# FP4 rounding from exponent bits, and one pass of each feed-forward pair on GpSimd

## The chip, the core and the metric

The kernel runs on one core of a Trainium2 chip. The metric is the device time of the whole kernel in microseconds. Before the change it took 3304.03 us (median of 3 runs, 3299.87 to 3309.81).

## What is computed

The kernel computes two layers of a small network on 4 x 1024 tokens of width 128. The change concerns the feed-forward part of layer 0, which works on FP4 values:

```python
_GRID = [0.0, 0.5, 1.0, 1.5, 2.0, 3.0, 4.0, 6.0]
_MID = [0.25, 0.75, 1.25, 1.75, 2.5, 3.5, 5.0]
def fp4_quant_dequant(x):                  # blocks of 16 along the last dimension
    xb = x.reshape(shape[:-1] + (shape[-1] // BLOCK, BLOCK))
    scale = jnp.max(jnp.abs(xb), axis=-1, keepdims=True) / 6.0
    scale = jnp.maximum(scale, 1e-12)
    xn = xb / scale
    idx = jnp.searchsorted(_MID, jnp.abs(xn))
    q = _GRID[idx] * jnp.sign(xn) * scale
...
gate = fp4_linear(x, w_gate)               # both operands are quantized
y = fp4_linear(x, w_up)
h = jax.nn.silu(gate) * y                  # 352 hidden values a token
return fp4_linear(h, w_down)
```

The input x is the layer-normed hidden state. Around this stand a gated delta-rule attention (layer 0), a causal attention and a mixture of eight experts (layer 1).

## The kernel before

The program is written out engine by engine, with semaphores between the engines; each engine works through its instructions in the written order, and nothing is planned at run time. Stages end in `end_phase`, where every engine drains and waits for all others. Everything that changes lies in the first stage.

The 4096 tokens lie as 32 tiles of 128 (tokens on the partitions), so `xn` and `xq` are 128 x 4096. VectorE normalizes x (`layernorm`), then quantizes all of x in one call of `quantize` (L562) into `xq`, raises `xq_done`, and quantizes the weights (`wraw`, 128 x 1120) into `wqt` in a second call. For x, ScalarE has written the sizes and signs into `fa` and `fsg`; for the weights VectorE makes them itself (L2174 to L2177). Once `xq_done` is up, GpSimd clears `bias3` with a memset (L1599) and splits the bias (L1602 to L1606); it has no other work until the next stage.

TensorE turns the weights (L1698, L1701) and then works through 16 pairs of tiles. For pair p: transposes of `xn` and `xq` (L1711, L1713), ScalarE's copies of them (L1982, L1983), the matmuls of gate and up (L1720, the gate half first), ScalarE's silu of the gate (L1986), VectorE's product with up (`hid`, L2187), the quantization of `hid` on VectorE into `hq` (128 x 704), with sizes and signs from ScalarE (L1991, L1994), the transposes of `hq` (L1747), ScalarE's copies (L2011, L2012), the down matmuls (L1753), and the addition into the residual `res` (L2191, `add_down`). The gate logits of the next stage ride along (L1729, L1732, copied at L1998, L1999).

The order is staggered by one pair: TensorE does gate and up of pair p+1 ahead of turning `hq` of pair p, and VectorE adds pair p-1's result into `res` inside the quantization of pair p, ahead of the sign product. After the second to last pair, VectorE adds the biases for the gates (L2212, L2214) and ScalarE computes a sigmoid over all gate logits and a root (L2019 to L2023), with two loads of function tables; it does so after its copies of that pair's turned hidden values.

`quantize` takes 13 passes: maximum of each block, scale, reciprocal, product with the reciprocal (L571), comparison with 5.0 (L573), two fused comparisons and additions (L575), doubling (L576), four more comparisons (L578), product with half the sign (L580), product with the scale (L581). Each pass waits for the one before by a semaphore (`link`).

Of the kernel before, what the change touches and what calls it, by code (L numbers as in the profile page):

```python
# [10 lines left out]
ALU = mybir.AluOpType  # L11
# [23 lines left out]
LEVELS = 3  # L35

# [25 lines left out]
def layer_kernel(nc, a, out):  # L62

    ctx = ExitStack()
    with ctx:
# [56 lines left out]
        fsg = sb("fsg", [P, T * D], scope=s1)  # L122
# [1467 lines left out]
        def _(pool):  # L1590
# [15 lines left out]
            split.done(pool.tensor_copy(bias_h[:, 2, :], bias_r[:, 1, :]))  # L1606
            end_phase(pool)
# [85 lines left out]
        def _(pe):  # L1693
# [11 lines left out]
            def gate_up(p):  # L1705
# [8 lines left out]
                last.then_inc(x_turned, 1)  # L1714
                pe.wait_ge(xT_done, 2 * p + 2)
# [19 lines left out]
            gate_up(0)  # L1735
            gate_logits(0)
            for p in range(FP):
                if p + 1 < FP:
                    gate_up(p + 1)
                    gate_logits(p + 1)  # L1740
                pe.wait_ge(hq_done, p + 1)
                pe.wait_ge(hT_done, 2 * p)
                pe.wait_ge(ffn_added, p)
                for y in range(2):
                    for c in range(3):
                        w = min(P, INNER - P * c)
# [219 lines left out]
        def _(act):  # L1966
            act.wait_ge(var_done, 1)
            act.activation(stats[:, 0, :], stats[:, 1, :], ACT.Sqrt).then_inc(std_done, 1)
            act.wait_ge(norm_done, 1)
            act.activation(fa[:, :], xn[:, :, :].rearrange("p t d -> p (t d)"), ACT.Abs).then_inc(sign_done, 1)  # L1970
            act.activation(fsg[:, :], xn[:, :, :].rearrange("p t d -> p (t d)"), ACT.Sign).then_inc(sign_done, 1)
# [7 lines left out]
            def begin_pair(p):  # L1979
# [3 lines left out]
                act.copy(xnT[:, 2 * P * p:2 * P * p + 2 * P], bank[0][:, 0:2 * P]).then_inc(xT_done, 1)  # L1983
                act.wait_ge(gu_done, 2 * p + 1)
# [3 lines left out]
            def sizes(p):  # L1988
                act.wait_ge(hid_done, p + 1)
                act.wait_ge(hq_done, p)  # L1990
                act.activation(fa[:, 0:2 * INNER], hid[:, :, :].rearrange("p y w -> p (y w)"), ACT.Abs).then_inc(hsign_done, 1)  # L1991

            def signs(p):
                act.activation(fsg[:, 0:2 * INNER], hid[:, :, :].rearrange("p y w -> p (y w)"), ACT.Sign).then_inc(hsign_done, 1)  # L1994
# [6 lines left out]
            begin_pair(0)  # L2001
            sizes(0)
            signs(0)
            keep_logits(0)
            for p in range(FP):
                if p + 1 < FP:
                    begin_pair(p + 1)
                    sizes(p + 1)
                act.wait_ge(h_turned, p + 1)
                act.wait_ge(down_done, p)  # L2010
                act.copy(hqT[:, :, 0:2, :], turn2[:, :, 0:2 * P].rearrange("p y (c w) -> p y c w", c=2)).then_inc(hT_done, 1)  # L2011
                act.copy(hqT[0:INNER - 2 * P, :, 2, :], turn2[0:INNER - 2 * P, :, 2 * P:3 * P]).then_inc(hT_done, 1)  # L2012
                if p + 1 < FP:
                    signs(p + 1)
# [146 lines left out]
        def _(dve):  # L2161
# [5 lines left out]
            quantize(dve, seq, xf, T * D // BLOCK, fa[:, :], fc[:, :], fsg[:, :], fsc,  # L2167
                     xq[:, :, :].rearrange("p t d -> p (t d)"),
                     lambda: dve.wait_ge(sign_done, 1), lambda: dve.wait_ge(sign_done, 2)).then_inc(xq_done, 1)
# [3 lines left out]
            wneg = fa[:, NW:2 * NW]  # L2173
            seq.link(dve.tensor_scalar(wneg, wraw[:, :], 0.0, None, ALU.is_lt))  # L2174
            seq.link(dve.scalar_tensor_tensor(out=fsg[:, 0:NW], in0=wraw[:, :], scalar=0.0, in1=wneg,
                                              op0=ALU.is_gt, op1=ALU.subtract))
            seq.link(dve.tensor_tensor(fa[:, 0:NW], wraw[:, :], fsg[:, 0:NW], ALU.mult))  # L2177
            quantize(dve, seq, wraw[:, :], NW // BLOCK, fa[:, 0:NW], fc_top, fsg[:, 0:NW], fsc,
                     wqt[:, :], lambda: None, lambda: None).then_inc(wq_done, 1)
# [3 lines left out]
            def hidden(p):  # L2183
                dve.wait_ge(silu_done, p + 1)
                dve.wait_ge(gu_done, 2 * p + 2)
                dve.wait_ge(hsign_done, 2 * p)
# [7 lines left out]
            for p in range(FP):  # L2194
                dve.wait_ge(hid_done, p + 1)
                dve.wait_ge(hq_done, p)

                def sign_ready():
                    if p:
                        add_down(p - 1)  # L2200
                    dve.wait_ge(hsign_done, 2 * p + 2)

                def abs_ready():
                    dve.wait_ge(hsign_done, 2 * p + 1)
                    dve.wait_ge(h_turned, p)
                quantize(dve, ffn, hid[:, :, :].rearrange("p y w -> p (y w)"), 2 * INNER // BLOCK, fa[:, 0:2 * INNER], fc_top[:, 0:2 * INNER],
                         fsg[:, 0:2 * INNER], fsc, hq[:, :, :].rearrange("p y w -> p (y w)"), abs_ready, sign_ready).then_inc(hq_done, 1)
# [330 lines left out]
```

## Time and profile before

| | |
|---|---|
| median of the timed runs | 3304.03 us |
| span of the profiled execution | 3302.8 us |
| VectorE busy | 2513.2 us (76%) |
| TensorE busy | 2799.4 us (85%) |
| ScalarE busy | 1627.2 us (49%) |
| GpSimd busy | 1339.6 us (41%) |

The page's busy times are averages over all stages. The stage of the change is the first one and ends near 323 us. The page states one time for the profiled execution, its span; the three timed runs are other executions. A busy time adds up the durations of instructions; consecutive linked instructions start 0.03 us after the one before has ended, and an instruction that does not wait for the one before it can start before that one's end.

### The profile page before, as it was taken

How to read it: one execution, taken by the hardware profiler on the slowest of the kernel's cores; microseconds unless marked ns; L12 is line 12 of the kernel's file. 1: busy time of each engine (PE TensorE's matmuls, PEld its weight loads, DVE VectorE, ACT ScalarE, POOL GpSimd, SP SyncE). 2: the span in 40 equal slices, each digit the busy share in tenths (PEclk: the TensorE clock that was granted, in tenths of full speed). 3: DMA queues.
4: the chain of work that ended last, by engine and by line, in shares of the span. 5: the costliest groups of instructions: out<-in, count | busy, mean ns of one | idle time of the engine just before them, and what ended most of it. 6: DMA issues, size and time to landing. Idle time of an engine off the chain costs nothing. (4 is left out here: it accounts for less than half of the span.)

```text
span 3302.8 us, 74706 instructions
## 1 busy us (share of the span) xinstructions
PE 2799.4 (85%) x27685; PEld 1932.7 (59%) x27685; DVE 2513.2 (76%) x4548; ACT 1627.2 (49%) x3792; POOL 1339.6 (41%) x2151
## 2 busy tenths in 40 slices
PE   0466999675999999999999999999867488888888
PEld 0354444464777777777777777777656372222223
DVE  8898788794787868788687877876577467877775
ACT  1233999684434334443434334344366355555555
POOL 0000223312565655656566565655564504311111
PEclk9887999897999999999999999999889689999999
DMA  1000665686123242232323233133187321111111
GB/s 58 1 0 24 227 237 239 250 267 158 34 75 67 44 86 62 57 68 69 52 67 81 43 77 70 43 73 70 44 279 226 126 55 36 35 24 21 20 28 28
DMA packets 487649, 290.82 MB, mean 88 GB/s; under 512 B 402899, under 2 KB 447507, under 8 KB 478483
## 3 DMA queue, kind: packets, MB, share of 16 engines
q1 hardware_dynamic: 478070, 256.64, 28.8%
q10 hardware_dynamic: 4608, 16.78, 1.6%
q0 software_dynamic: 4608, 12.59, 1.1%
q8 instruction: 225, 3.69, 0.5%
q14 instruction: 138, 1.13, 0.1%
HBM read 155.92 MB, written 129.99 MB: 87 GB/s over the span
## 5 line engine op out<-in xcount | busy, mean ns | idle before, releaser
L2457 DVE TENSOR_REDUCE mx<-banks 128x2 f32<-128x1024 f32 (+3 forms) x384 | 358.2, 956 | 106.5 <-PE banks L1882 84.9
L2148 ACT ACTIVATE probs<-banks 128x1024 f32<-128x1024 f32 (+3 forms) x384 | 306.9, 810 | 246.1 <-PE banks L1904 239.1
L1131 ACT COPY xs<-banks 64x64 f32<-64x64 f32 (+2 forms) x640 | 166.1, 260 | 397.3 <-PE banks L963 394.2
L832 POOL TENSOR_SCALAR xc<-xc,halves 128x64 f32<-128x64 f32 (+1 forms) x256 | 192.3, 751 | 360.9 <-DVE xc L1311 348.3
L1686 POOL TENSOR_SCALAR_AFFINE_SELECT probs<-probs 128x256 f32<-128x256 f32 x256 | 103.7, 407 | 523.9 <-ACT probs L2148 523.7
L963 PE MATMUL banks<-xc,ssm 64*64 64x16 f32 (+2 forms) x5120 | 250.3, 217 | 36.5 <-issue 34.6
L963 PEld LDWEIGHTS banks<-xc,ssm 64*64 64x64 f32 x5120 | 209.8, 135 | 115.8 <-issue 57.0
L1761 PE MATMUL banks<-wproj,xnT 128*128 128x512 f32 x512 | 265.3, 600 | 0.6 <-DVEq L484 0.6
L1311 DVE SCALAR_TENSOR_TENSOR xc<-xc,halves,banks 64x64 f32<-64x64 f32 (+1 forms) x512 | 159.9, 312 | 111.5 <-PE banks L974 105.4
L1121 ACT COPY ssm<-banks 16x64 f32<-16x64 f32 (+2 forms) x896 | 215.9, 241 | 50.8 <-PE banks L935 38.6
L1156 ACT COPY ah<-banks 128x768 f32<-128x768 f32 x128 | 102.2, 798 | 254.8 <-PE banks L995 254.8
L1620 POOL TENSOR_TENSOR prj_sq<-prj 128x1024 f32<-128x1024 f32 x32 | 77.5, 2423 | 368.6 <-ACT prj L2032 368.6
L995 PE MATMUL banks<-stk,tw 128*128 128x192 f32 x1024 | 204.8, 344 | 0.5 <-DVE tw L1309 0.5
L1904 PE MATMUL banks<-q_less,k_parts 64*128 64x512 bf16 (+3 forms) x768 | 134.0, 346 | 80.8 <-DVE mx L2457 61.2
L1921 PE MATMUL banks<-probs,vaug 128*9 128x256 f32 (+3 forms) x1920 | 195.7, 449 | 0.0
L985 PE MATMUL banks<-S_t,kqt 64*128 64x128 f32 x2048 | 184.6, 299 | 0.3 <-issue 0.3
L839 POOL TENSOR_TENSOR ag<-ah,gt_sb 128x512 f32<-128x512 f32 x128 | 162.9, 1273 | 49.7 <-ACT ah L1156 49.5
L995 PEld LDWEIGHTS banks<-stk,tw 128*128 128x128 f32 x1024 | 166.2, 193 | 16.0 <-DVE tw L1309 0.7
L974 PE MATMUL banks<-xs,ttw 64*64 64x32 f32 (+1 forms) x3072 | 171.2, 224 | 0.5 <-ACT xs L1131 0.5
L1147 ACT ACTIVATE nycv<-banks 128x512 f32<-128x512 f32 x128 | 76.4, 597 | 181.3 <-PE banks L985 181.3
L974 PEld LDWEIGHTS banks<-xs,ttw 64*64 64x64 f32 x3072 | 139.3, 135 | 44.3 <-ACT xs L1131 43.8
L1761 PEld LDWEIGHTS banks<-wproj,xnT 128*128 128x128 f32 x512 | 96.6, 192 | 98.5 <-issue 48.1
(361 smaller groups left out, 6768.5 us busy)
## 6 DMA issues: line engine op xcount, KB each, us to landing
proj_s<-prj SPq DMA_DIRECT2D x32, 2048.0 KB, 6.8
qkv_t<-proj_s SPq DMA_DIRECT2D x32, 1536.0 KB
ka<-proj_s ACTq DMA_DIRECT2D x32, 512.0 KB, 4.8
mem_s<-o_sb SPq DMA_DIRECT2D x32, 512.0 KB, 2.6
om<-mem_s SPq DMA_DIRECT2D x32, 512.0 KB, 3.9
om<-proj_s SPq DMA_DIRECT2D x32, 512.0 KB, 4.8
nblk_s<-ssa POOLq DMA_DIRECT2D x32, 256.0 KB, 4.6
blk_s<-res SPq DMA_DIRECT2D x16, 512.0 KB, 4.0
```

Source lines behind the costliest of these rows:

```text
L832: pool.tensor_scalar(inverse_of(k, lv + 1)[:, :, w:2 * w], inverse_of(k, lv), halves[:, lv, 1:2], None, ALU.mult).then_inc(half_set, 1)
L839: pool.tensor_tensor(ag[:, :, :], ah[:, k % 2, :, 0:P], gt_sb[:, k % 2, :, :], ALU.mult).then_inc(ag_set, 1)
L963: last = pe.matmul(products(k, lv, out_)[right, w * m:w * m + w], ssm[rows, lv, m, right], inverse_of(k, lv)[rows, m, :], start=True, stop ...
L974: last = pe.matmul(updates(k, lv, out_)[right, w * m:w * m + w], turned[right, right], xs[right, k % 2, w * m:w * m + w], start=True, stop ...
L985: last = pe.matmul(cols(bk[2 + m % 2], 2 * w + p), kqt[r, k % 2, p, w, :], S_t[r, 2 * g + p, :], start=(w == 0 and p == 0), stop=(w == 0), ...
L995: last = pe.matmul(cols(bk[p], m % 2, P + DK), tw[:, k % 2, m, :], stk[:, k % 2, m, :], start=True, stop=True)
L1121: last = act.copy(ssm[rows, lv, :, right].rearrange("p (k e) t -> p e k t", e=2), both[rows, :, :, right])
L1131: last = act.copy(xs[right, k % 2, 0:4 * (SUB << lv)], products(k, lv, out_)[right, :])
L1761: pe.matmul(bank[n], xnT[:, P * i:P * i + P], wproj[:, 512 * n:512 * n + 512], start=True, stop=False)
L1921: last = pe.matmul(bank[6][row:row + SLOT, n0 * P:512], vaug[:, b * TB + j, 2 * (s % 8) + e, :], p_, start=(j == 0), stop=(j == 6 + odd))
L2148: act.activation(probs[:, s % 2, :, at:at + w], slot_of((kind, s, k))[:, :, 0:w], ACT.Exp, scale=D1 ** -0.5).then_inc(b_read, 1)
L2457: dve.tensor_reduce(mx[:, s % 2, c, :, t:t + 1].rearrange("p e a -> p (e a)"), slot_of((kind, s, k))[:, :, 0:w], AX, ALU.max).then_inc(a_r ...
```

## The change

A new function `round_blocks` takes the place of `quantize`. It multiplies the signed value by 1/scale and by a constant just under 1 (so that ties go down), takes the exponent bits of the result with a bitwise AND, which gives a power of two, takes the larger of that and 1.0 times 1.5 * 2^22, adds this number and subtracts it again. The addition rounds to the grid of the number's binade. No size and no sign is needed, so ScalarE's Abs and Sign go, and VectorE's three passes for the weights' signs. The product with the scale is a function of its own, `scaled`. For x and the weights it stays on VectorE; for the pairs GpSimd does it. `fa` and the scales get two halves for this, used in turn. The semaphore `hsign_done` now says that a pair's rounding is done.

The order in the loop changes too. TensorE goes: turn `hq` of pair p-1, gate and up of p+1, down of p-1, turn x of p+2, gate logits of p+1. VectorE adds the residual of pair p-1 after the rounding of p. ScalarE's block of sigmoid and root keeps its place at the end of turn p = FP-2, but the copies of that pair's turned hidden values are now in the turn after it.

```diff
+I32 = mybir.dt.int32
+EXPONENT = 0x7F800000
+ROUNDER = 1.5 * 2 ** 22
+TIES_DOWN = 1.0 - 2.0 ** -22
...
-        def quantize(dve, c, src, n, a_, acc, sgn, sc, dst, abs_ready, sign_ready):
+        def round_blocks(dve, c, src, n, y, step, sc):
...
             c.link(dve.reciprocal(inv, scale))
-            abs_ready()
-            c.link(dve.tensor_tensor(blocks(a_), blocks(a_), inv.unsqueeze(2).to_broadcast([P, n, BLOCK]), ALU.mult))
-
-            c.link(dve.tensor_scalar(acc, a_, 5.0, 2.0, ALU.is_gt, ALU.mult))
-            for mid in (3.5, 2.5):
-                c.link(dve.scalar_tensor_tensor(out=acc, in0=a_, scalar=mid, in1=acc, op0=ALU.is_gt, op1=ALU.add))
-            c.link(dve.tensor_scalar(acc, acc, 2.0, None, ALU.mult))
-            for mid in (1.75, 1.25, 0.75, 0.25):
-                c.link(dve.scalar_tensor_tensor(out=acc, in0=a_, scalar=mid, in1=acc, op0=ALU.is_gt, op1=ALU.add))
-            sign_ready()
-            c.link(dve.scalar_tensor_tensor(out=acc, in0=acc, scalar=0.5, in1=sgn, op0=ALU.mult, op1=ALU.mult))
-            return dve.tensor_tensor(blocks(dst), blocks(acc), scale.unsqueeze(2).to_broadcast([P, n, BLOCK]), ALU.mult)
+            c.link(dve.scalar_tensor_tensor(out=blocks(y), in0=blocks(src), scalar=TIES_DOWN, in1=inv.unsqueeze(2).to_broadcast([P, n, BLOCK]), op0=ALU.mult, op1=ALU.mult))
+            c.link(dve.tensor_scalar(step.bitcast(I32), y.bitcast(I32), EXPONENT, None, ALU.bitwise_and))
+            c.link(dve.tensor_scalar(step, step, 1.0, ROUNDER, ALU.max, ALU.mult))
+            c.link(dve.tensor_tensor(y, y, step, ALU.add))
+            return dve.tensor_tensor(y, y, step, ALU.subtract)
+
+        def scaled(eng, y, n, sc, dst):
...
+            return eng.tensor_tensor(blocks(dst), blocks(y), sc[:, 0, 0:n].unsqueeze(2).to_broadcast([P, n, BLOCK]), ALU.mult)
...
 # GpSimd, behind the splitting of the bias
+            for p in range(FP):
+                pool.wait_ge(hsign_done, p + 1)
+                pool.wait_ge(h_turned, p)
+                scaled(pool, pair_of(fa, p), NPB, scales_of(p), hq[:, :, :].rearrange("p y w -> p (y w)")).then_inc(hq_done, 1)
...
 # TensorE
-            gate_up(0)
-            gate_logits(0)
-            for p in range(FP):
-                if p + 1 < FP:
-                    gate_up(p + 1)
-                    gate_logits(p + 1)
...
+            turn_x(0)
+            gate_up(0)
+            turn_x(1)
+            gate_logits(0)
+            for p in range(FP + 1):
+                if p >= 1:
+                    turn_hidden(p - 1)
+                if p + 1 < FP:
+                    gate_up(p + 1)
+                if p >= 1:
+                    down(p - 1)
+                if p + 2 < FP:
+                    turn_x(p + 2)
+                if p + 1 < FP:
+                    gate_logits(p + 1)
...
 # ScalarE
-            act.wait_ge(norm_done, 1)
-            act.activation(fa[:, :], xn[:, :, :].rearrange("p t d -> p (t d)"), ACT.Abs).then_inc(sign_done, 1)
-            act.activation(fsg[:, :], xn[:, :, :].rearrange("p t d -> p (t d)"), ACT.Sign).then_inc(sign_done, 1)
...
+            keep_x(0)
+            gate(0)
+            keep_x(1)
             keep_logits(0)
-            for p in range(FP):
+            for p in range(FP + 1):
+                if p >= 1:
+                    keep_hidden(p - 1)
                 if p + 1 < FP:
+                    gate(p + 1)
+                if p + 2 < FP:
+                    keep_x(p + 2)
                 if p + 1 < FP:
-                    signs(p + 1)
                     keep_logits(p + 1)
                 if p == FP - 2:
                     act.wait_ge(g_raw, 2 * FP)
...
 # VectorE
+                if p >= 2:
+                    dve.wait_ge(hq_done, p - 1)
+                round_blocks(dve, ffn, hid[:, :, :].rearrange("p y w -> p (y w)"), NPB, pair_of(fa, p), fc_top[:, 0:PAIR], scales_of(p)).then_inc(hsign_done, 1)
+                if p:
+                    add_down(p - 1)
                 if p + 1 < FP:
                     hidden(p + 1)
```

## Rows read from the trace of the kernel before

**Rows 1.** Windows: busy of PE, PEld, DVE, ACT, POOL; granted clock; DMA share; GB/s.

```profile
180.00:240.00 60.00, 42.48 (x176) 31.47 (x176) 57.60 (x80) 19.93 (x45) 0.00 (x0) 0.74 0.00 1
...
229.00:230.00 1.00, 1.00 (x6) 0.70 (x4) 0.97 (x2) 0.62 (x1) 0.00 (x0) 0.50 0.06 16
```

**Rows 2.** Timeline of VectorE, x: start, duration, operation, count, idle before.

```profile
33.95 4.41 DVE L567 TENSOR_REDUCE fsc<-xn 128x256 f32<-128x4096 f32 x1
...
40.51 4.43 DVE L571 TENSOR_TENSOR fa<-fa,fsc 128x4096 f32<-128x4096 f32 x1
44.97 2.29 DVE L573 TENSOR_SCALAR fc<-fa 128x4096 f32<-128x4096 f32 x1
```

**Rows 3.** Timelines of VectorE and TensorE, the weights.

```profile
85.37 4.06 DVE L2174 TENSOR_SCALAR fa<-wraw 128x1120 f32<-128x1120 f32 x1
...
92.19 1.32 DVE L567 TENSOR_REDUCE fsc<-wraw 128x70 f32<-128x1120 f32 x1
...
94.40 1.33 DVE L571 TENSOR_TENSOR fa<-fa,fsc 128x1120 f32<-128x1120 f32 x1
95.76 0.74 DVE L573 TENSOR_SCALAR fc<-fa 128x1120 f32<-128x1120 f32 x1
...
108.30 1.51 PE L1698 MATMUL banks<-ident,wqt 128*128 128x128 f32 x6 [108.30 <-DVE wqt L581]
```

**Rows 4.** GpSimd: two rows of its timeline, two of its groups by form.

```profile
85.33 3.51 POOL L1599 MEMSET bias<- 128x4096 bf16 x1 [82.41 <-DVE xq L581]
...
333.12 1.89 POOL L1620 TENSOR_TENSOR prj_sq<-prj 128x1024 f32<-128x1024 f32 x1 [240.30 <-ACT prj L2032]
...
L846 POOL TENSOR_TENSOR nycv<-cf,qkv_t 128x512 f32<-128x512 f32 x128 | 135.3, 1057 | 0.0
...
L832 POOL TENSOR_SCALAR xc<-xc,halves 128x64 f32<-128x64 f32 x128 | 115.2, 900 | 12.6
```

**Rows 5.** Timeline of VectorE in the loop of pairs.

```profile
118.96 0.89 DVE L2187 TENSOR_TENSOR hid<-silu_g,banks 128x704 f32<-128x704 f32 x1 [10.80 <-PE banks L1720]
...
202.00 0.42 DVE L2191 TENSOR_TENSOR res<-res,banks 128x256 f32<-128x256 f32 x1
...
204.07 0.88 DVE L2187 TENSOR_TENSOR hid<-silu_g,banks 128x704 f32<-128x704 f32 x1
204.99 0.89 DVE L567 TENSOR_REDUCE fsc<-hid 128x44 f32<-128x704 f32 x1
...
206.59 0.89 DVE L571 TENSOR_TENSOR fa<-fa,fsc 128x704 f32<-128x704 f32 x1
207.52 0.53 DVE L573 TENSOR_SCALAR fc<-fa 128x704 f32<-128x704 f32 x1
```

**Rows 6.** Timeline of TensorE in the loop of pairs.

```profile
211.09 4.52 PE L1720 MATMUL banks<-wguT,xqT 128*128 128x352 f32 x8 [0.73 <-ACT xnT L1983]
...
216.40 0.88 PE L1747 MATMUL banks<-ident,hq 128*128 128x128 f32 x6
218.76 1.61 PE L1753 MATMUL banks<-wdT,hqT 128*128 128x128 f32 x12 [1.48 <-ACT hqT L2012]
...
221.54 2.63 PE L1720 MATMUL banks<-wguT,xqT 128*128 128x352 f32 x8 [0.74 <-ACT xnT L1983]
...
228.60 1.54 PE L1747 MATMUL banks<-ident,hq 128*128 128x128 f32 x6 [3.64 <-DVE hq L581]
```

**Rows 7.** Timelines of VectorE, ScalarE and TensorE at the end of the stage.

```profile
301.60 0.88 DVE L2187 TENSOR_TENSOR hid<-silu_g,banks 128x704 f32<-128x704 f32 x1
...
322.64 0.42 DVE L2191 TENSOR_TENSOR res<-res,banks 128x256 f32<-128x256 f32 x1 [5.51 <-PE banks L1753]
...
305.94 1.28 ACT L2019 ACT_TABLE_LOAD   x1 [0.87 <-DVE bgate L2214]
...
312.77 0.63 ACT L2023 ACTIVATE sb_tok<-sb_tok 128x512 f32<-128x512 f32 x1
...
319.67 2.93 PE L1753 MATMUL banks<-wdT,hqT 128*128 128x128 f32 x12 [0.94 <-ACT hqT L2012]
```

More of the change, by code:

```diff
@@ L121, in layer_kernel @@
         fa = sb("fa", [P, T * D], scope=s1)
-        fsg = sb("fsg", [P, T * D], scope=s1)
+        above_fa = sb("above_fa", [P, T * D], scope=s1)
         fsc = sb("fsc", [P, 2, T * D // BLOCK], scope=s1)
@@ L569, in quantize, with blocks, pair_of, scales_of @@
             c.link(dve.reciprocal(inv, scale))
-            abs_ready()
-            c.link(dve.tensor_tensor(blocks(a_), blocks(a_), inv.unsqueeze(2).to_broadcast([P, n, BLOCK]), ALU.mult))
-            c.link(dve.tensor_scalar(acc, a_, 5.0, 2.0, ALU.is_gt, ALU.mult))
-            for mid in (3.5, 2.5):
-                c.link(dve.scalar_tensor_tensor(out=acc, in0=a_, scalar=mid, in1=acc, op0=ALU.is_gt, op1=ALU.add))
-            c.link(dve.tensor_scalar(acc, acc, 2.0, None, ALU.mult))
-            for mid in (1.75, 1.25, 0.75, 0.25):
-                c.link(dve.scalar_tensor_tensor(out=acc, in0=a_, scalar=mid, in1=acc, op0=ALU.is_gt, op1=ALU.add))
-            sign_ready()
-            c.link(dve.scalar_tensor_tensor(out=acc, in0=acc, scalar=0.5, in1=sgn, op0=ALU.mult, op1=ALU.mult))
-            return dve.tensor_tensor(blocks(dst), blocks(acc), scale.unsqueeze(2).to_broadcast([P, n, BLOCK]), ALU.mult)
+            c.link(dve.scalar_tensor_tensor(out=blocks(y), in0=blocks(src), scalar=TIES_DOWN, in1=inv.unsqueeze(2).to_broadcast([P, n, BLOCK]), op0=ALU.mult, op1=ALU.mult))
[4 more added lines that the diff above has]
+        def scaled(eng, y, n, sc, dst):
+            def blocks(x):
+                return x.rearrange("p (n k) -> p n k", k=BLOCK)
+            return eng.tensor_tensor(blocks(dst), blocks(y), sc[:, 0, 0:n].unsqueeze(2).to_broadcast([P, n, BLOCK]), ALU.mult)
+        PAIR = 2 * INNER
+        NPB = PAIR // BLOCK
+        def pair_of(buf, p):
+            return buf[:, PAIR * (p % 2):PAIR * (p % 2) + PAIR]
+        def scales_of(p):
+            return fsc[:, :, NPB * (p % 2):NPB * (p % 2) + NPB]
         PT = T // 8
@@ L1703, in _, with turn_x @@
             pe.wait_ge(wT_done, 3)
-            def gate_up(p):
+            def turn_x(p):
                 if p == 0:
@@ L1714, in gate_up @@
                 last.then_inc(x_turned, 1)
+            def gate_up(p):
                 pe.wait_ge(xT_done, 2 * p + 2)
@@ L1733, in gate_logits, with turn_hidden @@
                 last.then_inc(g_mm, 1)
-            gate_up(0)
-            gate_logits(0)
-            for p in range(FP):
-                if p + 1 < FP:
-                    gate_up(p + 1)
-                    gate_logits(p + 1)
+            def turn_hidden(p):
                 pe.wait_ge(hq_done, p + 1)
@@ L1748, in _, with down @@
                 last.then_inc(h_turned, 1)
+            def down(p):
                 pe.wait_ge(hT_done, 2 * p + 2)
@@ L1977, in _, with keep_x @@
             act.copy(wdT[0:INNER - 2 * P, 2, :], bank[2][0:INNER - 2 * P, 2 * P:3 * P]).then_inc(wT_done, 1)
-            def begin_pair(p):
+            def keep_x(p):
                 act.wait_ge(x_turned, p + 1)
@@ L1983, in begin_pair, with gate @@
                 act.copy(xnT[:, 2 * P * p:2 * P * p + 2 * P], bank[0][:, 0:2 * P]).then_inc(xT_done, 1)
+            def gate(p):
                 act.wait_ge(gu_done, 2 * p + 1)
@@ L1986, in begin_pair, with keep_hidden @@
                 act.activation(silu_g[:, :, :], gate2, ACT.Silu).then_inc(silu_done, 1)
[L1988 to L1994, printed above, removed]
+            def keep_hidden(p):
+                act.wait_ge(h_turned, p + 1)
+                act.wait_ge(down_done, p)
+                act.copy(hqT[:, :, 0:2, :], turn2[:, :, 0:2 * P].rearrange("p y (c w) -> p y c w", c=2)).then_inc(hT_done, 1)
+                act.copy(hqT[0:INNER - 2 * P, :, 2, :], turn2[0:INNER - 2 * P, :, 2 * P:3 * P]).then_inc(hT_done, 1)
             def keep_logits(p):
@@ L2166, in _ @@
             xf = xn[:, :, :].rearrange("p t d -> p (t d)")
-            quantize(dve, seq, xf, T * D // BLOCK, fa[:, :], fc[:, :], fsg[:, :], fsc,
-                     xq[:, :, :].rearrange("p t d -> p (t d)"),
-                     lambda: dve.wait_ge(sign_done, 1), lambda: dve.wait_ge(sign_done, 2)).then_inc(xq_done, 1)
+            seq.link(round_blocks(dve, seq, xf, T * D // BLOCK, fa[:, :], fc[:, :], fsc))
+            scaled(dve, fa[:, :], T * D // BLOCK, fsc, xq[:, :, :].rearrange("p t d -> p (t d)")).then_inc(xq_done, 1)
             dve.wait_ge(ld1, 112)
             dve.wait_ge(xq_done, 1)
[L2173 to L2179, printed above, removed]
+            seq.link(round_blocks(dve, seq, wraw[:, :], NW // BLOCK, fa[:, 0:NW], fc_top, fsc))
+            scaled(dve, fa[:, 0:NW], NW // BLOCK, fsc, wqt[:, :]).then_inc(wq_done, 1)
             dve.wait_ge(wq_done, 1)
@@ L2185, in hidden @@
                 dve.wait_ge(gu_done, 2 * p + 2)
-                dve.wait_ge(hsign_done, 2 * p)
                 dve.tensor_tensor(hid[:, :, :], silu_g[:, :, :], up2, ALU.mult).then_inc(hid_done, 1)
@@ L2195, in _ @@
                 dve.wait_ge(hid_done, p + 1)
[L2196 to L2207, printed above, removed]
+                if p >= 2:
[3 more added lines that the diff above has]
+                    add_down(p - 1)
                 if p + 1 < FP:
```

9 lines of the change are left out of this document (removed).

## The prediction

> **What bounds the kernel now.** I read the table by windows first, for the shape of the first stage, then each engine's timeline inside it, and last the end of that stage. From 180 to 240 us VectorE is busy 57.60 of 60 us, TensorE 42.48, ScalarE 19.93 and GpSimd nothing at all [rows 1]. The feed-forward loop is VectorE's. Its first `hid` product starts at 118.96 [rows 5] and its sixteenth at 301.60 [rows 7]: 182.64 us for 15 pairs, 12.18 us each. TensorE waits for it: in the turn of the loop from 216.40 to 228.60 (12.20 us) it stands idle 1.48 + 0.74 + 3.64 = 5.86 us and works 6.34 us [rows 6]. Ahead of the loop VectorE is alone: quantizing x from 33.95 to 85.37 [rows 2, 3], the weights until TensorE starts at 108.30 [rows 3]. What VectorE drops in this stage is therefore on the path, until TensorE, or the way DVE -> GpSimd -> TensorE -> DVE, is as long. The later stages keep their instructions and start when this one has ended on all engines, so a gain here should reach the end whole.
>
> Durations come from one execution whose span is 3302.8 us; the profile's page gives no other time for it. The median of the three timed runs is 3304.0, so 1.2 us lie around the span or between runs; I take the saving off the span and add the 1.2 back.
>
> **x (4096 elements a partition).** Before: 85.37 - 33.95 = 51.42 us. After: maximum, scale and reciprocal stay, 40.51 - 33.95 = 6.56; the fused multiply by 1/scale and by the tie constant 4.46 (4.43 and 0.03 to the next linked start [rows 2]); the AND and the max-times-constant 2 x 2.33, as the one-source form at 2.29 [rows 2]; add and subtract 2 x 4.46; the product with the scale 4.46. Sum 29.1. Saved 22.3. ScalarE's Abs and Sign on x lay beside it and give nothing.
>
> **Weights (1120 elements).** Before: 108.30 - 85.37 = 22.93. After, without disturbance: maximum to reciprocal 94.40 - 92.19 = 2.21, fused multiply, add, subtract, scale 4 x 1.35 = 5.4, and two one-source passes at 0.77 [rows 3]: 9.15. But the first row of this group took 4.06 us, where the same form and size takes 0.74 [rows 3]: it ended with the 3.51 us memset that GpSimd began at 85.33 [rows 4]. After the change the memset is still released by `xq_done`; the maximum (1.32) can run beside it, and then a one-source pass of 70 elements comes at +1.35 and, if it is held in the same way, gets through at about +3.5. That adds 2.2: 11.3. Saved 11.6 (13.8 if it is not held).
> The Trainium skill, "SBUF — State Buffer", section "Who interferes with whom", states the rule behind such a hold: a VectorE instruction in a two-port mode, or one with two SBUF inputs against a GpSimd instruction that reads SBUF, and the GpSimd instruction lock each other out, and whoever comes first keeps the port. By it the sum is as above with the hold; this row agrees. It also speaks against moving a pass to GpSimd, which I price below.
>
> **A pair on VectorE (704 elements).** What is left, by starts: `hid` product 0.92 (204.07 to 204.99), maximum to reciprocal 1.60 (204.99 to 206.59), fused multiply 0.93 (206.59 to 207.52), AND and max-times-constant 2 x 0.56 (0.53 and 0.03), add 0.92; then subtract and the residual add together 1.15, which is 204.07 - 202.00 = 2.07 less one linked pass of 0.92 [rows 5]. Sum 6.64. Gone: six comparisons, one doubling, the sign product, and the scale product, which goes to GpSimd.
> The AND on int32 has no row. Bounds: 0.53 (one-source pass) and 0.89 (two-source pass) [rows 5]; I take 0.53, the nearer form, one source and 4-byte data; the other end costs 0.36 x 16 + 2.1 + 0.6 = 8.5 us. Below 0.53 nothing in the rows points.
> The Trainium skill ("VectorE: DVE Perf Modes", section "What auto-detection actually checks") picks that faster mode by where the operands lie and how many sources there are, which would give 0.53; no run here shows it for an integer operation.
>
> **The pass on GpSimd.** 704 elements, two inputs, the scale broadcast over runs of 16. Rows: 1024 elements in 1.89 us alone; 512 in 1.06 with broadcast operands [rows 4]. Between them 704 give 1.3 to 1.5; I take 1.5. Beside it VectorE does the residual add and the `hid` product (one operand in PSUM) and the maximum (one source), 0.34 + 0.92 + 0.92 = 2.2 us, so the first instruction that could be held comes after the pass is over. Low end 1.3; high end, if the 1.06 us were all a price per run (8 runs of 64, 0.132 each), 44 runs x 0.132 = 5.8 us.
>
> **The ring through TensorE.** From the end t of a pair's rounding: hand-over 0.05, pass 1.5, hand-over 0.05, transposes 0.88 (GpSimd's product is now ahead of them), gate and up of the pair after next 2.47 (2.63 with its tail), down 1.61 [rows 6]: 6.6 us. ScalarE's copies of the turned hidden values (0.94 where TensorE waits for them [rows 7]) fall under gate and up. The residual add of that pair stands on VectorE after the next rounding, at about t + 6.6. The two are equal, so VectorE waits next to nothing; each 1 us more in the ring costs 0.5 us a pair, because one turn of the ring holds two roundings' worth. TensorE needs 6.34 or less of the period. I take 6.7 us a pair. Queued behind a late residual add on VectorE are the `hid` product and the next rounding, and behind that product TensorE's gate and up.
> The clock: TensorE was granted 0.50 of its clock (1.2 GHz) from 229 to 230 [rows 1], just after 3.64 us of idle time, and after idle times of 1.48 and 0.74 its matmuls still took the short durations of 2.4 GHz (down 1.61 against 2.93, gate and up 2.63 against 4.52) [rows 6, 7]. After the change the idle time is 0.4 to 0.7 us a pair, so it should stay high. Once, at the beginning, it will not: pair 0's transposes come some 8.0 us after the first `hid` starts, 3 us after TensorE ran dry, and 8.0 + 1.54 + 4.5 + 1.6 (transposes and gate and up at the low clock, down at the high one) ends at 15.7, where VectorE is through with the second rounding at 6.3 + 0.9 + 5.4 = 12.6: the first residual add is about 3.1 us late.
> First `hid` to sixteenth: 6.3 (no residual add) + 14 x 6.7 + 3.1 = 103.2, against 182.64. Saved 79.4. The 10.7 us from 108.30 to the first `hid` (weights turned, first gate and up) stay.
>
> **The end of the stage.** Before, 322.64 + 0.42 - 301.60 = 21.5 us from the sixteenth `hid` (s) to the last residual add [rows 7]. After: sb_tok and bias sums at s+0.9 to s+1.8, rounding 15 until s+7.2. But ScalarE's sigmoid and root block (305.94 to 313.40, 7.5 us [rows 7]) now stands ahead of its copies for pair 14, not behind them: it runs s+1.8 to s+9.3, copies to s+10.3, down 2.93 at the low clock to s+13.2, residual add, transposes 1.54, copies 0.95, down 2.93, residual add: s+19.6. Saved only 1.9: ScalarE's order gives back here what two roundings would have brought.
>
> **Sum.** 22.3 + 11.6 + 79.4 + 1.9 = 115.2. Span 3187.6, time 3188.8, called 3189.
>
> **Rivals.**
> A. TensorE stays at 1.2 GHz in the loop, because the new rhythm has some idle time in every pair. For: the granted clock is 0.74 on average over these 60 us [rows 1], so many turns before run at the low clock. Against: those follow 3.6 us of idle time. TensorE is then the bound: transposes 1.54, gate and up 4.52, down 2.93, and for turning x and the gate logits what 6.34 leaves at full clock (6.34 - 0.88 - 2.63 - 1.61 = 1.2), or up to twice that [rows 6, 7]: 10.2 to 11.4, near 10.5: 14 x 3.8 - 3.1 = +50, 3239.
> B. GpSimd's pass costs by runs, up to 5.8 us, and holds VectorE's passes too. For: a 64-element pass there takes 0.90 us [rows 4], so size alone does not price it. Against: the 8-run row at 1.06. Ring 10.9, period (10.9 + 6.64)/2 = 8.8: +29, 3218.
> C. Slower than before: the ring does not overlap at all. Where the residual add is one pair behind the rounding there are two pairs under way; if each pair had to go round before the next rounding could end, the idle time on TensorE would pull its clock down too, and a pair costs 1.6 + 1.54 + 4.7 + 2.93 + 0.42 + 0.92 + 5.4 = 17.5 us. 15 x 5.3 = 80 lost against 34 won ahead of the loop: 3350. It decides from 14.6 us a pair. Against: every wait of the loop names a pair at least one behind.
> D. The AND at one element a cycle: 3197.
>
> **Numbers.** Forecast with its small unknowns, D and both ends of the hold and the first stall (3180 to 3205): 0.70. B, in full or in part (3205 to 3222): 0.13. A, in full or in part: 0.13. C: 0.02; no measurable change, by nothing I can name: 0.02. For 8 in 10 the range takes in B and the near part of A, 3178 to 3226. A measurement of this kernel tells 0.3% (10 us) from no change; faster 0.96, same 0.02, slower 0.02.
>
> **What would show it.** Right: `xq_done` near 63 us; TensorE's first transpose near 74; 6.6 to 6.8 us between `hid` products; GpSimd passes of 1.3 to 1.6 us; TensorE over 85% busy in the loop at the granted clock 1.00; about 8 us in which ScalarE's copies for pair 14 wait for the sigmoid block; the stage ending near 208. Wrong: one-source int32 passes of 0.9 us; VectorE idle before the residual adds by over 1 us each; GpSimd passes over 2.2 us, or small VectorE passes stretched beside them; a granted clock of 0.5 to 0.8 in the loop; or a later stage that has grown.

## The result, and the profile after

| | before | after |
|---|---|---|
| median of the timed runs | 3306.92 us (4 runs, 3299.87 to 3310.89) | 3184.44 us (4 runs, 3180.49 to 3187.86) |
| span of the profiled execution | 3302.8 us | 3185.7 us |
| first `hid` product starts | 118.96 | 84.66 |
| sixteenth `hid` product starts | 301.60 | 183.84 |
| first matmul of the next stage | 323.17 | 203.50 |

The ratio of the times is 0.9637 (95% interval 0.9619 to 0.9655). 3189 was forecast, with 3178 to 3226 as the range. The stage of the change ends 119.7 us earlier; 115.2 were forecast. The medians differ by 122.5 us. The span fell by 117.1, so the unchanged stages behind the first took 2.6 us more in this pair of executions, of which more below.

The timelines of VectorE and, in the last line, of TensorE after the change, up to the first `hid`; they answer to [rows 2, 3] (columns as there):

```profile
34.03 4.41 DVE L577 TENSOR_REDUCE fsc<-xn 128x256 f32<-128x4096 f32 x1
...
45.05 2.29 DVE L581 TENSOR_SCALAR fc<-fa 128x4096 int32<-128x4096 int32 x1
...
63.16 1.32 DVE L577 TENSOR_REDUCE fsc<-wraw 128x70 f32<-128x1120 f32 x1
64.52 2.15 DVE L578 TENSOR_SCALAR fsc<-fsc 128x70 f32<-128x70 f32 x1
...
84.66 0.89 DVE L2214 TENSOR_TENSOR hid<-silu_g,banks 128x704 f32<-128x704 f32 x1 [10.38 <-PE banks L1744]
...
74.43 1.51 PE L1719 MATMUL banks<-ident,wqt 128*128 128x128 f32 x6 [74.43 <-DVE wqt L589]
```

x takes 63.16 - 34.03 = 29.1 us instead of 51.4, and the weights 74.43 - 63.16 = 11.3 instead of 22.9 (74.43 is TensorE's first transpose). The AND on int32 costs what a one-source pass in float32 costs, 2.29 us. The pass over the weights' 70 scales reads 2.15 us and ends when GpSimd's memset does (next fence: 63.10 + 3.51 = 66.61). This is the hold that [rows 3, 4] showed.

The timelines of GpSimd, VectorE and TensorE after the change, the last two over one turn of the loop; they answer to [rows 4 to 6]:

```profile
63.10 3.51 POOL L1616 MEMSET bias<- 128x4096 bf16 x1 [60.18 <-DVE xq L589]
...
150.51 1.38 POOL L589 TENSOR_TENSOR hq<-fa,fsc 128x704 f32<-128x704 f32 x1 [5.25 <-DVE fa L584]
```

```profile
144.04 0.88 DVE L2214 TENSOR_TENSOR hid<-silu_g,banks 128x704 f32<-128x704 f32 x1
...
147.49 0.53 DVE L581 TENSOR_SCALAR fc<-fa 128x704 int32<-128x704 int32 x1
...
149.54 0.89 DVE L584 TENSOR_TENSOR fa<-fa,fc 128x704 f32<-128x704 f32 x1
150.35 0.41 DVE L2218 TENSOR_TENSOR res<-res,banks 128x256 f32<-128x256 f32 x1
150.68 0.88 DVE L2214 TENSOR_TENSOR hid<-silu_g,banks 128x704 f32<-128x704 f32 x1
```

```profile
145.31 0.88 PE L1767 MATMUL banks<-ident,hq 128*128 128x128 f32 x6 [0.83 <-POOL hq L589]
...
148.39 1.50 PE L1776 MATMUL banks<-wdT,hqT 128*128 128x128 f32 x12
...
151.95 0.88 PE L1767 MATMUL banks<-ident,hq 128*128 128x128 f32 x6 [0.83 <-POOL hq L589]
```

VectorE has no idle time here, and a turn takes 150.68 - 144.04 = 6.64 us. The ring ends in time: down is over at 148.39 + 1.50 = 149.89, the residual add starts at 150.35 behind the subtraction. GpSimd's pass takes 1.38 us. TensorE's only wait in the turn is 0.83 us, and its matmuls have the short durations.

The windows of the same stretch (columns as in [rows 1]):

```profile
120.00:160.00 40.00, 35.02 (x218) 28.74 (x217) 38.32 (x61) 16.45 (x44) 8.30 (x6) 1.00 0.00 1
```

TensorE is busy 35.02 of 40 us, at the full granted clock, where it was 42.48 of 60 at 0.74.

The end of the stage, timelines of VectorE, ScalarE and TensorE, answering to [rows 7]:

```profile
190.17 0.89 DVE L584 TENSOR_TENSOR fa<-fa,fc 128x704 f32<-128x704 f32 x1
...
202.97 0.42 DVE L2218 TENSOR_TENSOR res<-res,banks 128x256 f32<-128x256 f32 x1 [5.57 <-PE banks L1776]
```

```profile
185.75 1.28 ACT L2053 ACT_TABLE_LOAD   x1 [1.42 <-DVE bgate L2234]
...
192.59 0.63 ACT L2057 ACTIVATE sb_tok<-sb_tok 128x512 f32<-128x512 f32 x1
193.12 0.57 ACT L2029 COPY hqT<-banks 128x512 f32<-128x512 f32 x1
```

```profile
185.11 0.87 PE L1767 MATMUL banks<-ident,hq 128*128 128x128 f32 x6 [1.27 <-POOL hq L589]
194.01 2.93 PE L1776 MATMUL banks<-wdT,hqT 128*128 128x128 f32 x12 [8.02 <-ACT hqT L2030]
```

VectorE has rounded its last pair at 191.06. Pair 14's values were turned at 185.98, but ScalarE copies them only at 193.12, behind its sigmoid and root; TensorE's down waits 8.02 us for them. From the sixteenth `hid` to the next stage 19.7 us pass, where it was 21.6.

### The profile page after: what moved, and what is told of

Its sections match the earlier page's. It is cut to its first block and busy times, and to the rows that moved or that the text cites. A ratio compares the mean times of both kernels' runs of the same rounds, so it can differ in the third digit from the quotient of the medians.

```text
span 3185.7 us, 74542 instructions
## 1 busy us (share of the span) xinstructions
PE 2756.1 (87%) x27685; PEld 1909.2 (60%) x27685; DVE 2394.1 (75%) x4439; ACT 1599.3 (50%) x3758; POOL 1359.5 (43%) x2167
## 5 line engine op out<-in xcount | busy, mean ns | idle before, releaser
L1012 PEld LDWEIGHTS banks<-stk,tw 128*128 128x128 f32 x1024 | 167.9, 194 | 16.1 <-DVE tw L1326 0.7
L952 PE MATMUL banks<-kqt 64*128 64x256 f32 x1024 | 149.0, 411 | 0.0
```

The source lines that it names most:

```text
L1012: last = pe.matmul(cols(bk[p], m % 2, P + DK), tw[:, k % 2, m, :], stk[:, k % 2, m, :], start=True, stop=True)
```

## Experiments

All are edits of the changed kernel unless said otherwise. "Stage" is the start of the next stage's first matmul in the profiled execution, "a pair" the mean distance of the sixteen `hid` products. Each ratio is to the kernel before as it was timed beside that kernel, so it can differ a little from the quotient of two medians of this table.

| kernel | median us | ratio to before (95%) | a pair | stage |
|---|---|---|---|---|
| before | 3306.92 | 1 | 12.18 | 323.17 |
| after | 3184.44 | 0.9637 (0.9619 to 0.9655) | 6.61 | 203.50 |
| scale_on_vector | 3198.07 | 0.9687 (0.9665 to 0.9708) | 7.54 | 216.71 |
| round_only | 3195.30 | 0.9678 (0.9658 to 0.9698) | 7.88 | 218.57 |
| order_only | 3292.03 | 0.9966 (0.9951 to 0.9980) | 11.24 | 307.20 |
| down_last | 3192.73 | 0.9669 (0.9642 to 0.9696) | 7.24 | 213.29 |
| port_read | 3190.90 | 0.9657 (0.9634 to 0.9681) | 7.26 | 214.79 |
| sigmoid_later | 3180.83 | 0.9616 (0.9594 to 0.9638) | 6.79 | 201.64 |
| weights_first | 3175.27 | 0.9606 (0.9584 to 0.9628) | 6.70 | 196.28 |
| both_moves | 3174.33 | 0.9608 (0.9589 to 0.9627) | 6.72 | 190.91 |
| after_again | 3187.47 | 0.9644 (0.9626 to 0.9662) | 6.72 | 204.62 |
| weights_first_2 | 3180.38 | 0.9610 (0.9597 to 0.9624) | 6.80 | 197.81 |
| both_moves_2 | 3172.80 | 0.9598 (0.9583 to 0.9613) | 6.80 | 192.88 |

**The scale product back on VectorE.**

```diff
-            for p in range(FP):           # GpSimd
-                pool.wait_ge(hsign_done, p + 1)
-                pool.wait_ge(h_turned, p)
-                scaled(pool, pair_of(fa, p), ...).then_inc(hq_done, 1)
...
+                ffn.link(round_blocks(dve, ffn, ...))
+                dve.wait_ge(h_turned, p)
+                scaled(dve, pair_of(fa, p), ...).then_inc(hq_done, 1)
```

> The changed kernel, with the pairs' product with the scale back on VectorE, behind the rounding; order of the loop as after the change. My theory: the loop is bound by VectorE's own instructions (6.63 us from one hid product to the next), so the pass costs its 0.92 us in each of 15 periods and nothing at the end of the stage, where ScalarE's sigmoid block decides: 7.55 us a pair, +13.9 us, 3198. Rival (the ring through GpSimd and TensorE sets the pace, VectorE's length does not): the ring loses two hand-overs and 0.5 us, so the time stays or falls, 3180 to 3184.

Measured: 3198.1, a pair 7.54 us, stage 13.2 us later. The loop is bound by VectorE's own instructions; the pass moved to GpSimd is worth 0.92 us a pair. A window of two microseconds and TensorE's timeline show something more:

```profile
146.00:148.00 2.00, 2.00 (x5) 1.25 (x5) 1.86 (x5) 0.85 (x2) 0.00 (x0) 0.50 0.00 0
```

```profile
137.91 2.60 PE L1740 MATMUL banks<-wguT,xqT 128*128 128x352 f32 x8
...
144.67 1.47 PE L1763 MATMUL banks<-ident,hq 128*128 128x128 f32 x6 [1.60 <-DVE res L2214]
145.93 3.64 PE L1740 MATMUL banks<-wguT,xqT 128*128 128x352 f32 x8
...
190.02 0.85 PE L1763 MATMUL banks<-ident,hq 128*128 128x128 f32 x6 [1.60 <-DVE res L2214]
```

Around 1.60 us of idle time the clock fell here to 0.50, gate and up took 3.64 instead of 2.60, and nothing was lost: the ring had that much room. Nine turns of this loop have 1.59 or 1.60 us of idle time ahead of the transposes of `hq`. In four of them gate and up took 3.64 or 4.30 us, in the other five, the last line's among them, 2.60.

**The new rounding in the old order** (the kernel before, with `round_blocks` and `scaled` on VectorE for x, weights and pairs, no Abs and Sign; every engine's order as before, with the residual add ahead of the product with the scale).

```diff
-                quantize(dve, ffn, hid..., abs_ready, sign_ready).then_inc(hq_done, 1)
+                ffn.link(round_blocks(dve, ffn, hid..., NPB, fa[:, 0:PAIR], fc_top[:, 0:PAIR], scales_of(0)))
+                if p:
+                    add_down(p - 1)
+                dve.wait_ge(h_turned, p)
+                scaled(dve, fa[:, 0:PAIR], NPB, scales_of(0), hq...).then_inc(hq_done, 1)
```

> The kernel before, with the new rounding alone: order of all engines as before, product with the scale on VectorE. My theory: TensorE's old order puts everything of a pair in series (transposes 0.88, ScalarE's copies 0.94 to 1.48, down 1.61, turning x 0.6, ScalarE's copies 0.74, gate and up 2.47, gate logits 0.9), 8.1 to 8.6 us, longer than VectorE's 7.56; so 8.3 us a pair: 15 x 1.67 = +25 against the changed kernel, less about 4 at the end of the stage, where ScalarE's copies for pair 14 come ahead of the sigmoid block again: about 3205. Rival (VectorE's instructions alone decide): 7.56 us a pair, 3184 + 13.9 - 4 = 3194. In both the part ahead of the loop is as short as after the change.

Measured: 3195.3, a pair 7.88 us (7.84 in the middle), stage 218.57. Timelines of TensorE and VectorE:

```profile
148.14 0.85 PE L1762 MATMUL banks<-ident,hq 128*128 128x128 f32 x6
149.93 1.60 PE L1768 MATMUL banks<-wdT,hqT 128*128 128x128 f32 x12 [0.94 <-ACT hqT L2013]
...
152.71 2.63 PE L1735 MATMUL banks<-wguT,xqT 128*128 128x352 f32 x8 [0.74 <-ACT xnT L1995]
...
155.98 0.85 PE L1762 MATMUL banks<-ident,hq 128*128 128x128 f32 x6
```

```profile
147.62 0.89 DVE L2180 TENSOR_TENSOR hid<-silu_g,banks 128x704 f32<-128x704 f32 x1 [0.19 <-PE banks L1735]
...
155.45 0.89 DVE L2180 TENSOR_TENSOR hid<-silu_g,banks 128x704 f32<-128x704 f32 x1 [0.19 <-PE banks L1735]
```

TensorE never waits for `hq` (no idle time at 155.98); it waits only for ScalarE's copies, 0.94 and 0.74 us a turn, and sets the pace: the mechanism of my theory. Its size was off, 8.3 against 7.84, as I had taken the copies' wait between 0.94 and 1.48 and counted the tails of matmuls that overlap. VectorE waits only 0.19 us a pair, so it is nearly level with TensorE, and the median lies nearer to the rival's 3194 than to my 3205; it is the two timelines, and not the time, that tell the two apart. So of the 12.18 us a pair, 4.3 go with the rounding alone, and the new order with GpSimd's pass brings 1.3 more. Over the whole stage the rounding alone is worth 104.6 of the 119.7 us. The end of the stage is 16.1 us here, since ScalarE's copies for pair 14 come first.

**The old comparisons in the new order** (the old rounding for x, weights and pairs, sizes and signs of x and pairs on ScalarE again, the pairs' scale product on GpSimd).

```diff
-                round_blocks(dve, ffn, hid..., NPB, pair_of(fa, p), fc_top[:, 0:PAIR], scales_of(p)).then_inc(hsign_done, 1)
+                quantize(dve, ffn, hid..., NPB, fa[:, 0:PAIR], pair_of(fc[:, T * D // 2:], p), fsg[:, 0:PAIR], scales_of(p), None, ...).then_inc(hsign_done, 1)
```

> The changed kernel's order, with the pass on GpSimd, but the old comparisons as rounding (sizes and signs from ScalarE again, weights' signs on VectorE). My theory: VectorE bound, 12.19 - 0.92 = 11.27 us a pair, everything ahead of the loop as long as before: against the kernel before 15 x 0.92 = -13.8 and about -2 to +2 at the end of the stage, so 3290 to 3294. Rival (the new order is where most of the gain comes from): well under 3270.

Measured: 3292.0, ratio 0.9966 (0.9951 to 0.9980), a pair 11.24 (11.27 expected), stage 16.0 us earlier than before. While VectorE is the bound, the new order with GpSimd's pass is worth the pass that leaves VectorE, 0.94 us a pair, and 1.4 us at the end of the stage.

**Down behind the gate logits.**

```diff
                 if p + 1 < FP:
                     gate_up(p + 1)
-                if p >= 1:
-                    down(p - 1)
                 if p + 2 < FP:
                     turn_x(p + 2)
                 if p + 1 < FP:
                     gate_logits(p + 1)
+                if p >= 1:
+                    down(p - 1)
```

> The changed kernel, with TensorE's down of pair p-1 put behind turning x of p+2 and the gate logits of p+1: no work is added, the ring through TensorE is 1.31 us longer. It has 0.42 us of slack now (down ends at 149.89, the residual add starts at 150.35 with a hand-over of 0.04), so the residual add would be 0.89 late, of which one period bears half: 7.08 us a pair, 14 x 0.44 = +6.2, 3190.6. Rival 1 (slack hides it, VectorE alone decides): +0. Rival 2 (the ring closes on every pair, so the whole of it shows): 14 x 0.89 = +12.5, 3197.

Measured: 3192.7. Timeline of VectorE over two turns:

```profile
144.49 0.88 DVE L2214 TENSOR_TENSOR hid<-silu_g,banks 128x704 f32<-128x704 f32 x1
...
151.15 0.88 DVE L2214 TENSOR_TENSOR hid<-silu_g,banks 128x704 f32<-128x704 f32 x1
...
158.32 0.42 DVE L2218 TENSOR_TENSOR res<-res,banks 128x256 f32<-128x256 f32 x1 [0.79 <-PE banks L1776]
158.66 0.88 DVE L2214 TENSOR_TENSOR hid<-silu_g,banks 128x704 f32<-128x704 f32 x1
```

The turns alternate: 6.66 us without a wait and 7.51 us with 0.79 of idle time ahead of the residual add, together 7.09 a pair (7.08 expected). That is the half: the delay falls on one turn in two. Rival 1 (no effect) is refuted by the idle time; rival 2 would have shown a wait in every turn. The mean of 7.24 over all pairs includes 4.0 us of wait at the first residual add. The time alone (+8.3, with intervals of 6 us either way on the one kernel and 9 on the other) would not have told the theory from either rival.

**A second pass on GpSimd, to meet VectorE's small pass.**

```diff
                 scaled(pool, pair_of(fa, p), ..., hq...).then_inc(hq_done, 1)
+                pool.wait_ge(sign_done, p)
+                scaled(pool, fa[:, 2 * PAIR:3 * PAIR], NPB, scales_of(p), above_fa[:, 0:PAIR]).then_inc(sign_done, 1)
...
                 if p >= 2:
                     dve.wait_ge(hq_done, p - 1)
+                    dve.wait_ge(sign_done, p - 1)
```

> The changed kernel, with a second pass of the same form (704 elements, into a scratch tile) on GpSimd behind the first; hq_done is raised by the first, so the ring is as long as before, and the output is the same. Theory (a GpSimd instruction and a VectorE instruction that use the port they share lock each other out for their whole length): the second pass runs from 1.45 to 2.85 us behind the rounding's end, and VectorE's pass over the 44 scales (0.18 us, a one-source form of the kind that the memset held) is due at 2.1; it is held for 0.8 us, every period is 7.4 us, +12, 3196, and that pass reads some 1.0 us in the profile. Rival (GpSimd's work is free whatever it meets): +0, 3184.

Measured: a pair 7.21 us in the middle, stage 11.3 us later, 3190.9. Timelines of GpSimd and VectorE:

```profile
150.50 1.38 POOL L589 TENSOR_TENSOR hq<-fa,fsc 128x704 f32<-128x704 f32 x1 [4.49 <-DVE fa L584]
151.84 1.38 POOL L589 TENSOR_TENSOR above_fa<-fa,fsc 128x704 f32<-128x704 f32 x1
```

```profile
151.58 0.89 DVE L577 TENSOR_REDUCE fsc<-hid 128x44 f32<-128x704 f32 x1
152.50 0.77 DVE L578 TENSOR_SCALAR fsc<-fsc 128x44 f32<-128x44 f32 x1
153.30 0.43 DVE L579 RECIPROCAL fsc<-fsc 128x44 f32<-128x44 f32 x1
```

The pass over 44 scales reads 0.77 us instead of 0.18 and ends at 153.27, when GpSimd's second pass does (153.22). The period grows by that, from 6.63 to 7.21. This is what the Trainium skill's rule ("SBUF — State Buffer", section "Who interferes with whom") says of a VectorE instruction in a two-port mode and a GpSimd instruction that holds the shared port. The maximum, which ran beside it from 151.58, kept its 0.89. The real pass is free only because it is over 0.6 us before that small one is due. The period is 7.21 and not 7.4, as the held pass ends 0.05 us after GpSimd's and not its own 0.18 after it, and as the second pass ran 0.06 us earlier than I had put it. Twelve such periods make 7.0 of the 11.3 us; the rest is 2.8 in the turn of the first residual add (0.9 of it the same hold, 1.80 a wait for TensorE), 1.2 at the end and 0.4 ahead of the loop. At the end GpSimd's second pass (1.83 us instead of 1.38) and VectorE's addition of the gates' bias (1.33 instead of 0.14) are both stretched.

The hold goes both ways, and the changed kernel shows it already while the weights are rounded. Timelines of VectorE and GpSimd there (`after`):

```profile
67.33 1.33 DVE L580 SCALAR_TENSOR_TENSOR fa<-wraw,fsc 128x1120 f32<-128x1120 f32 x1
...
67.46 1.29 POOL L1622 TENSOR_TENSOR bias_r<-bias_r,bias_h 128x32 f32<-128x32 f32 x1
```

GpSimd's instruction over 32 elements starts behind VectorE's, takes 1.29 us and ends 0.09 us after it; in weights_first, where VectorE is idle at that point, it takes 0.24.

**ScalarE's sigmoid block later.**

```diff
             for p in range(FP + 1):
                 if p >= 1:
                     keep_hidden(p - 1)
+                if p == FP - 1:
+                    ...                    # g_raw, g_bias, two sigmoids, root: moved here
...
-                if p == FP - 2:
-                    ...                    # from here
```

> The changed kernel, with ScalarE's block of sigmoid and root put behind the copies of pair 14's turned hidden values instead of ahead of them. My theory: the end of the stage waits for this block; from the sixteenth hid product to the last residual add it goes from 19.55 to 14.8 us: -4.7, 3179.7. Rival: the block is in the way of pair 15's copies then and nothing is won, 3184.

Measured: from the sixteenth `hid` to the next stage 201.64 - 186.83 = 14.8 us instead of 19.7. The block hardly delays pair 15's copies; the down matmuls wait 1.04 us for them, where they wait 0.94 in the changed kernel:

```profile
198.14 2.93 PE L1776 MATMUL banks<-wdT,hqT 128*128 128x128 f32 x12 [1.04 <-ACT hqT L2030]
```

So the end of the stage is 4.85 us shorter. The stage as a whole ends only 1.9 us earlier here, as the loop in this execution lost 2.7 us at its first residual add and had no such loss in `after`. The median is 3180.8, with an interval of 7 us either way that overlaps the changed kernel's, so the times don't show the saving. Timeline of TensorE at the first pair's transposes, here and then in the changed kernel:

```profile
92.86 1.54 PE L1767 MATMUL banks<-ident,hq 128*128 128x128 f32 x6 [2.89 <-POOL hq L589]
94.19 4.72 PE L1744 MATMUL banks<-wguT,xqT 128*128 128x352 f32 x8
```

```profile
92.58 0.88 PE L1767 MATMUL banks<-ident,hq 128*128 128x128 f32 x6 [3.02 <-POOL hq L589]
93.29 2.53 PE L1744 MATMUL banks<-wguT,xqT 128*128 128x352 f32 x8
```

**Weights ahead of x.**

```diff
+            # the seven transfers of wraw first, then
             for c in range(4):
                 sp.dma_start(res[:, 8 * c:8 * c + 8, :], ...).then_inc(ld, 16)
...
+            dve.wait_ge(ld1, 112)
+            seq.link(round_blocks(dve, seq, wraw[:, :], NW // BLOCK, fa[:, 0:NW], fc_top, fsc))
+            scaled(dve, fa[:, 0:NW], NW // BLOCK, fsc, wqt[:, :]).then_inc(wq_done, 1)
+            dve.wait_ge(wq_done, 1)
             dve.wait_ge(ld, 64)
             layernorm(dve, seq, res, xn, xnT, 0)
```

> The changed kernel, with the weights loaded ahead of x and quantized by VectorE ahead of the layer norm, in part while x is still on its way (VectorE idles for its first 10.5 us). VectorE is taken by the weights until about 17 instead of starting on x at 10.5, so xq_done comes about 6.5 us later (69.6), but the weights' 11.3 us with the memset's hold of about 2, and TensorE's and ScalarE's turning of the weights (3.5 us), are no longer behind it: first hid product at about 77 instead of 84.66, -7.7, 3176.7. Rival: x lands later because the weights' transfers go first, or the weights land late, and VectorE waits for it: -3 or less.

Measured: 3175.3. Timeline of VectorE:

```profile
7.34 1.32 DVE L577 TENSOR_REDUCE fsc<-wraw 128x70 f32<-128x1120 f32 x1 [7.34 <-DMA wraw<-in_w_down]
8.69 0.20 DVE L578 TENSOR_SCALAR fsc<-fsc 128x70 f32<-128x70 f32 x1
...
16.55 4.42 DVE L503 TENSOR_REDUCE stats<-res 128x32 f32<-128x4096 f32 x1
...
76.12 0.89 DVE L2214 TENSOR_TENSOR hid<-silu_g,banks 128x704 f32<-128x704 f32 x1 [7.13 <-PE banks L1744]
```

The weights land at 7.3, VectorE takes up x at 16.55 without waiting for it, and the small pass that the memset had stretched to 2.15 us reads 0.20. First `hid` at 76.12 instead of 84.66: 8.5 us.

**Both moves.** Both of the last two edits together, and the changed kernel again beside it; then the weights' move alone and both once more, side by side.

> The changed kernel, with both moves: the weights loaded and quantized ahead of x, and ScalarE's sigmoid block behind the copies of pair 14's turned hidden values. They lie at the two ends of the stage and share nothing, so the savings add: 9 from the weights (7.2 in the stage, 9 in the medians) and 4.8 at the end: 3184.4 less 12 to 14, 3171. Rival: with the weights' moves the memset and the splitting of the bias meet VectorE's passes later, or the spread of the later stages (8 us between executions) covers it: 3176 or more.

> The changed kernel once more, beside the one with both moves, on the same chip: 3184 as before, within its own spread of some 4 us; the first residual add waits between 0 and 3 us by TensorE's clock when the first pair's transposes start (0 in the first profile).

Measured: 3174.3 against 3187.5 on the same chip, stage 190.91 against 204.62, so 13.7 us in the stage and 13.1 in the medians (ratios 0.9608 and 0.9644, whose intervals just touch: 0.9589 to 0.9627 and 0.9626 to 0.9662). As weights_first alone had 3175.3 in another comparison, this left open whether the second move shows in the time:

> The kernel of weights_first once more, on the same chip as the one with both moves: the first comparison had them on different chips, 3175.3 and 3174.3, though in the profiles the stage with both moves ends 5.4 us earlier (190.91 against 196.28). If the two moves add in the time as they do in the stage, this one is 5 us slower than both_moves_2.

> The kernel with both moves once more, beside weights_first_2. If the moves add: 5 us faster than weights_first_2. If the later stages take the 5 us back (their order is the same, they only start earlier): the same time within 2 us.

Measured: 3180.4 and 3172.8, ratios to before 0.9610 (0.9597 to 0.9624) and 0.9598 (0.9583 to 0.9613), stage 197.81 and 192.88. In the stage the moves add (4.9 to 5.4 us). The medians differ by 7.6 us and the ratios by 0.0012, about 4 us, but the intervals overlap, so in the time it is likely and not shown. The kernel with both moves has the lowest medians of all that were tried, and the interval of its second run (0.9583 to 0.9613) lies clear of that of the changed kernel (0.9626 to 0.9662).

## Why the prediction was right

- **VectorE bounds the first stage, and what it drops is on the path**: right. scale_on_vector puts 0.92 us of it back and pays 0.92 a pair.
- **x, 22.3 us**: 51.42 - 29.13 = 22.3. **Weights, 11.6**: 22.93 - 11.27 = 11.7, with the memset's hold (2.15 - 0.20 us of it).
- **The AND at 0.53**: right (0.53 at 704 elements, 2.29 at 4096). Rival D is out.
- **A pass of 1.5 us on GpSimd**: 1.38. Rival B's price per run of 16 is out.
- **6.7 us a pair**: 6.64 between `hid` products in the middle, with VectorE never idle; the ring had 0.42 us of room where I had it level. From the rounding's end to the end of down it took 6.09 us where I had added up 6.56: GpSimd's pass is 0.12 shorter, down 0.11, and the transposes with gate and up take 3.08 instead of 3.35, as they overlap. That one turn bears half of a delay in the ring: shown by down_last.
- **3.1 us at the first residual add**: the term that was mis-sized, in this execution. It took 0. Pair 0's transposes came after 3.02 us of idle time and still ran at the full clock (0.88, gate and up 2.53). In other executions of kernels with the same instructions up to that point the same place went the other way: after 2.89 us of idle time 1.54 and 4.72 at half clock, and the residual add waited 2.65 us (sigmoid_later). In after_again the transposes kept the high clock, but gate and up behind them did not, and the residual add waited 1.53 us:

```profile
92.09 0.88 PE L1767 MATMUL banks<-ident,hq 128*128 128x128 f32 x6 [3.02 <-POOL hq L589]
92.81 4.22 PE L1744 MATMUL banks<-wguT,xqT 128*128 128x352 f32 x8
```

The four kernels with the weights first, whose loop is the same, waited 1.25, 1.53, 2.73 and 2.74 us. So the mechanism of the term shows in six of seven executions, always at less than 3.1 us, and the first profile is the one where it cost nothing. It is between 0 and 3 us, different in each execution, and no fixed cost.
- **The end, s + 19.6**: the last residual add ends at 203.39, s + 19.55. sigmoid_later shows that the block's place holds back 4.85 us.
- **Turning the weights to the first `hid`, 10.7**: 10.2, as the first gate and up took 4.70 us instead of 5.06.
- **Sum**: 119.7 instead of 115.2 in the stage; 4.0 of the difference lies in the loop (103.2 forecast, 99.2 measured), 3.1 of them at the first residual add. That the forecast time came as near as 4.6 us is in part luck: executions of one kernel differ by up to 15 us, more than any of these terms was off.
- **Later stages keep their time**: 2982.2 us instead of 2979.6, right within their own spread (2969.9 to 2988.3 in the profiles below).
- **Rival A** (half clock): the windows show 1.00. It is not far off, though: scale_on_vector had the half clock in four turns of its loop, at 1.60 us of idle time, and there the loop had room for it. **Rival C** (no overlap): VectorE has no idle time in the loop, so no turn waits for its own pair.

## What to carry to other kernels

Where a ring of waits closes two turns later, price it at half of its excess over the bounding engine's two turns (1/k for k turns by the same argument; only two are shown here), and read the slack from the trace (end of the last link against the start of what waits for it) before lengthening it. When a pass goes to GpSimd, list what VectorE does in that time: the pass was free here beside a residual add, a `hid` product and a maximum, and not beside the short pass over the scales. When the order of a loop is shifted by a turn, look at the one-time block at its end: its place relative to the other work shifts too.

## What the runs showed of the hardware that was not expected

The length of TensorE's idle time alone does not decide its clock. Six transposes of `hq` after 3.02 us of idle time took 0.88 us (after), after 2.89 us 1.54 (sigmoid_later), and after only 1.60 us 1.47 (scale_on_vector), where five other turns of the same execution kept the high clock after the same idle time. What else decides it no run here varied.

The spread between executions of one kernel comes mostly from behind the changed stage. The rest of the span, from the next stage's first matmul on, took 2982.2 us in `after`, 2969.9 in after_again, 2988.3 in sigmoid_later and 2971.3 in both_moves_2, with the same instructions. Windows of the same stretch behind the changed stage, first in sigmoid_later and then in both_moves_2:

```profile
700.00:1200.00 500.00, 488.52 (x5966) 395.31 (x5966) 383.59 (x911) 198.72 (x616) 294.86 (x514) 0.98 0.27 59
```

```profile
700.00:1200.00 500.00, 488.54 (x6083) 396.34 (x6085) 393.56 (x934) 201.94 (x626) 302.51 (x527) 1.00 0.28 62
```

TensorE is as busy in both, but the granted clock is 0.98 in one and 1.00 in the other, and fewer matmuls fit in (5966 against 6083, 2% less). Over whole executions the two go together as well: of 38 of the kernel before, timed beside the experiments, the seven with a mean granted clock of 0.941 have a mean span of 3308.5 us, the six with 0.946 3299.7, and the three with 0.947 3297.5. This fits a stage bound by TensorE whose clock is now and then lowered; no run here varied the clock by itself, so the cause is argued, not shown. A saving of 5 us in this kernel is seen in the stage's own rows and not in three timed runs.
